# A linear-attention and routed-FFN kernel: one semaphore for each constant and load in the setup, and another order of its steps

## The reference

```python
q, k, v = split(x @ w_qkv)                      # to heads: 16 x 8
q_proj = elu1(einsum('bhnd,hdf->bhnf', q, proj))   # elu1(t) = t + 1 if t > 0 else exp(t)
k_proj = elu1(einsum('bhnd,hdf->bhnf', k, proj))
kv = einsum('bhnf,bhnd->bhfd', k_proj, v)
attn = einsum('bhnf,bhfd->bhnd', q_proj, kv) / (q_proj . sum_n(k_proj) + 1e-8)
x = layernorm(x + attn @ w_out + b_out)
expert = argmax(x @ wr + br)
x = layernorm(x + gelu(x @ w1[expert] + b1[expert]) @ w2[expert] + b2[expert])
```

## Time and profile before

| | us |
|---|---|
| runs | 243.63, 241.59, 245.2; median 243.63 |
| the profiled execution, its own time | 242.73 |
| its span in the trace | 241.0 |
| TensorE busy | 194.7 (81% of the span) |
| VectorE busy | 166.7 (69%) |
| ScalarE busy | 141.9 (59%) |
| GpSimd busy | 127.5 (53%) |

### The profile page before, as it was taken

One profiled execution on the slowest core, in us unless ns is written; L12 is line 12 of the kernel. 1 busy time (PEld: TensorE's weight loads), 2 busy tenths in 40 slices (PEclk: granted clock), 3 DMA queues, 4 the chain that ended last, 5 costly groups with the idle time before them and its releaser, 6 DMA issues.

```text
span 241.0 us, 5866 instructions
## 1 busy us (share of the span) xinstructions
PE 194.7 (81%) x1685; PEld 155.3 (64%) x1685; DVE 166.7 (69%) x539; ACT 141.9 (59%) x374; POOL 127.5 (53%) x161
## 2 busy tenths in 40 slices
PE   0778999999989889778874958899999899999100
PEld 0467887887854535444450447789999899999100
DVE  0247769686737789999998696767777757775600
ACT  2238888787846574675473356677766576676000
POOL 8203829273630012665585363644888756668860
PEclk9979999999999999999998579999999999999855
DMA  5999999998910000100110076861777887751100
GB/s 142 244 412 415 411 414 407 409 412 285 239 35 0 0 1 4 45 22 22 48 35 22 34 189 211 240 188 39 215 203 224 236 246 207 217 151 45 36 6 0
DMA packets 28416, 40.45 MB, mean 168 GB/s; under 512 B 3497, under 2 KB 18126, under 8 KB 28384
## 3 DMA queue, kind: packets, MB, share of 16 engines
q1 hardware_dynamic: 26112, 35.80, 45.4%
q0 software_dynamic: 2272, 4.27, 5.1%
HBM read 17.95 MB, written 22.56 MB: 168 GB/s over the span
## 4 chain that ended last, share of the span: by engine, by line
PE 47%; POOL 16%; issue 13%; DVE 11%; ACT 6%; DMA 2%; SPq 2%; DVEq 1%; ACTq 0%; POOLq 0%
PE pair L290 13%; PE pair L695 10%; PE pair L708 6%; POOL out_dram L493 5%; POOL sorted_rows L474 5%; PE bank L580 4%; PE bank L708 2%; PE pair L646 2%; DMA x_all<-sorted_rows 2%; POOL rstd L457 2%; PE pair L637 2%; PE bank L637 1%; PE pair L549 1%; DVE qexp L909 1%; POOL rstd L489 1%
## 5 line engine op out<-in xcount | busy, mean ns | idle before, releaser
L843 ACT ACTIVATE qfeat<-pair,w_sb 128x128 f32<-128x128 f32 x156 | 44.8, 369 | 26.1 <-PE pair L695 25.4
L695 PE MATMUL pair<-xsT,w_slot 128*128 128x128 f32 x312 | 42.6, 281 | 2.5 <-ACT xsT L833 1.6
L474 POOL DMA_INDIRECT sorted_rows<-x,dest x32 | 31.9, 997 | 17.7 <-issue 11.2
L695 PEld LDWEIGHTS pair<-xsT,w_slot 128*128 128x128 f32 x312 | 38.7, 195 | 3.7 <-issue 3.7
L290 PE MATMUL pair<-wkv_part,xT_all 128*128 128x256 f32 x192 | 34.6, 328 | 3.0 <-DVE xT_all L901 1.6
L290 PEld LDWEIGHTS pair<-wkv_part,xT_all 128*128 128x128 f32 x192 | 29.5, 195 | 6.4 <-issue 6.4
L502 POOL TENSOR_TENSOR ksum<-kfeat 128x512 f32<-128x512 f32 x12 | 16.3, 1355 | 31.8 <-DVE kfeat L918 31.8
L290 PE MATMUL pair<-xT_all,wq_part 128*128 128x512 f32 x96 | 31.8, 456 | 0.0
L708 PE MATMUL pair<-w_sb,qfeat 128*128 x232 | 30.8, 276 | 0.0
L797 ACT ACTIVATE qexp<-pair,minus_one 128x512 f32<-128x512 f32 x32 | 20.7, 680 | 15.5 <-PE pair L290 15.5
L493 POOL DMA_INDIRECT out_dram<-x_all x26 | 26.0, 1000 | 7.0 <-issue 5.8
(11 more groups left out here) (159 smaller groups left out, 362.3 us busy)
## 6 DMA issues: line engine op xcount, KB each, us to landing
sorted_rows<-pad_rows SPq DMA_DIRECT2D x11, 1584.0 KB, 23.0
w_slot<-in_L_ffn_w_dram SPq DMA_DIRECT2D x39, 256.0 KB
x_all<-in_L_attn_x_dram SPq DMA_DIRECT2D x8, 256.0 KB, 3.7
w_sb<-in_L_ffn_w_dram SPq DMA_DIRECT2D x4, 512.0 KB, 13.7
x_all<-sorted_rows SPq DMA_DIRECT2D x26, 66.0 KB, 2.6
xs<-sorted_rows SPq DMA_DIRECT2D x13, 66.0 KB, 2.7
w_sb<-in_L_ffn_b_dram SPq DMA_DIRECT2D x1, 512.0 KB, 6.8
sorted_rows<-x,dest POOLq DMA_INDIRECT x32, 2.4
```

What stands on the lines that cost most here:

```text
L474: g_.indirect_dma_start(out=sorted_rows, out_offset=bass.IndirectOffsetOnAxis(ap=dest[:, ring, i:i + 1], axis=0), in_=x1[:, ring, i, :], i ...
L695: last = mm(h_bank[t % 2][:, k * P:(k + 1) * P], w1_slot[:, t % WB, k * P:(k + 1) * P], xsT[:, t % 2, :], start=True, stop=True)
L843: a_.activation(hT[:, t % 2, k * P:(k + 1) * P], h_bank[t % 2][:, k * P:(k + 1) * P], ACT.Gelu, bias=w2_sb[:, bass.ds(w_at[t] + (FF + D + ...
```

## The change

GpSimd's constants get semaphores of their own (`ones_ready`, `ident_ready`, `mask_ready`, `pads_ready`), and so do the loads (`w_in`, `proj_in`, `wr_in`, `wout_in`). What makes the keys' weights goes first on every engine: the head mask's selects stand ahead of the other constants, and the fills of `pad_rows` and `x1` behind all. The query weights, the output weights and `b1` go behind the turning of x group 0, and the two score products (L553, L554 in the kernel before) between tiles 0 and 1. TensorE begins with four matmuls of ones into PSUM that nobody reads (`keep_awake`), and makes a fifth behind the first transposes. The core of the diff:

```diff
@@ sync @@
-            sp.dma_start(wqkv_sb[:, :], w_qkv).then_inc(const_in, 16)
-            sp.dma_start(proj_sb[:, :], proj.rearrange("h d f -> (h d) f")).then_inc(const_in, 16)
             def load_x(g):
                 sp.dma_start(x_all[:, g * GT:(g + 1) * GT, :], x_groups[g]).then_inc(x_loaded[g], 16)
+            sp.dma_start(wqkv_sb[:, :], w_qkv).then_inc(w_in, 16)
+            sp.dma_start(proj_sb[:, :], proj.rearrange("h d f -> (h d) f")).then_inc(proj_in, 16)
+            sp.dma_start(wr_sb[:, :], wr).then_inc(wr_in, 16)
             load_x(0)
+            sp.dma_start(wout_sb[:, 0:D], w_out).then_inc(wout_in, 16)
+            sp.dma_start(bout_col[:, :], b_out.rearrange("(d a) -> d a", a=1)).then_inc(wout_in, 16)
+            sp.dma_start(b1_rows[:, :], b1.rearrange("e (c p) -> (e c) p", p=P)).then_inc(b1_in, 16)
             load_x(1)
-            sp.dma_start(wout_sb[:, 0:D], w_out).then_inc(const_in, 16)
             sp.dma_start(bout_sb[:, :], b_out.rearrange("(a d) -> a d", a=1).to_broadcast([P, D])).then_inc(const_in, 16)
-            sp.dma_start(wr_sb[:, :], wr).then_inc(const_in, 16)
             sp.dma_start(br_sb[:, :], br.rearrange("(a d) -> a d", a=1).to_broadcast([P, E])).then_inc(const_in, 16)
-            sp.dma_start(bout_col[:, :], b_out.rearrange("(d a) -> d a", a=1)).then_inc(const_in, 16)
-            sp.dma_start(b1_rows[:, :], b1.rearrange("e (c p) -> (e c) p", p=P)).then_inc(b1_in, 16)
             for g in range(2, G):
...
-            sp.wait_ge(pool_consts, 1)
+            sp.wait_ge(pads_ready, 1)
@@ gpsimd @@
+            g_.memset(ones_bf[:, :], 1.0)
+            g_.memset(share[:, :], 1.0 / P).then_inc(ones_ready, 1)
             g_.memset(ident[:, :], 1.0).then_inc(zeroed, 1)
-            g_.memset(before[:, :], 1.0).then_inc(zeroed, 1)
             g_.memset(head_mask[:, :], 1.0).then_inc(zeroed, 1)
-            g_.memset(ones_bf[:, :], 1.0)
-            g_.memset(ones_kv[:, :], 1.0)
             g_.memset(mean_of[:, :], 1.0 / D)
-            g_.memset(den_eps[:, :], DEN_EPS)
             g_.memset(zero[:, :], 0.0)
             g_.memset(minus_one[:, :], -1.0)
-            g_.memset(share[:, :], 1.0 / P)
+            g_.memset(den_eps[:, :], DEN_EPS)
+            pool.wait_ge(zeroed, 2)
+            g_.affine_select(out=ident[:, :], in_=ident[:, :], compare_op=ALU.is_equal, fill=0.0, base=0,
+                             pattern=[[-1, P]], channel_multiplier=1).then_inc(ident_ready, 1)
+            g_.affine_select(out=head_mask[:, :], in_=head_mask[:, :], compare_op=ALU.is_ge, fill=0.0, base=0,
+                             pattern=[[-HD, H]], channel_multiplier=1).then_inc(zeroed, 1)
             g_.memset(block_mask[:, :], 1.0).then_inc(zeroed, 1)
+            g_.memset(before[:, :], 1.0).then_inc(zeroed, 1)
+            pool.wait_ge(zeroed, 3)
+            g_.affine_select(out=head_mask[:, :], in_=head_mask[:, :], compare_op=ALU.is_ge, fill=0.0, base=HD - 1,
+                             pattern=[[HD, H]], channel_multiplier=-1).then_inc(mask_ready, 1)
...
+            g_.iota(region_up[:, :], pattern=[[CAP, E]], base=1 - P, channel_multiplier=0,
+                    allow_small_or_imprecise_dtypes=True).then_inc(pool_consts, 1)
+            g_.memset(pad_rows[:, :, :], 0.0).then_inc(zeroed, 1)
+            pool.wait_ge(zeroed, 8)
+            g_.iota(pad_rows[:, :, D:D + 1].bitcast(I32), pattern=[[0, PR], [0, 1]], base=NO_TOKEN, channel_multiplier=0).then_inc(pads_ready, 1)
+            g_.memset(x1[:, :, :, :], 0.0).then_inc(zeroed, 1)
@@ tensor @@
-            pe.wait_ge(pool_consts, 1)
-            pe.wait_ge(const_in, 16 * 7)
+            def keep_awake(n):
+                for _ in range(n):
+                    mm(bank[5][:, :], ones_bf[:, :], share[:, :].to_broadcast([P, 512]), start=True, stop=True)
+            pe.wait_ge(ones_ready, 1)
+            keep_awake(4)
+            pe.wait_ge(ident_ready, 1)
+            pe.wait_ge(w_in, 16)
             for i in range(2):
                 nc.tensor.transpose(bank[0][:, i * P:(i + 1) * P], wqkv_sb[:, i * D:(i + 1) * D], ident[:, :]).then_inc(w_turned, 1)
-            mm(bank[3][:, 0:E], mean_of[:, :], wr_sb[:, :], start=True, stop=True).then_inc(wr_mean, 1)
-            nc.tensor.transpose(bank[4][:, 0:P], wout_sb[:, 0:D], ident[:, :]).then_inc(wout_turned, 1)
-            pe.wait_ge(b1_in, 16)
-            nc.tensor.transpose(bank[6][:, 0:E * FC], b1_rows[:, :], ident[0:E * FC, 0:E * FC]).then_inc(b1_turned, 1)
+            keep_awake(1)
             pe.wait_ge(w_turn_kept, 1)
             pe.wait_ge(proj_ready, 1)
-            for i in (1, 0):
-                mm(bank[1 + i][:, :], wT[:, i, :], proj_diag[:, :, :].rearrange("p h f -> p (h f)"),
-                   start=True, stop=True).then_inc(w_feat_pre, 1)
-            pe.wait_ge(woutT_ready, 1)
-            pe.wait_ge(wr_mid_ready, 1)
-            mm(bank[5][:, 0:E], woutT[:, :], wr_mid[:, :], start=True, stop=True)
-            mm(bank[5][:, E:2 * E], bout_col[:, :].to_broadcast([P, P]), wr_mid[:, :], start=True, stop=True).then_inc(wout_pre, 1)
+            def feature_weights(i, out):
+                mm(out, wT[:, i, :], proj_diag[:, :, :].rearrange("p h f -> p (h f)"), start=True, stop=True).then_inc(w_feat_pre, 1)
+            feature_weights(1, bank[2][:, :])
+            pe.wait_ge(wr_in, 16)
+            mm(bank[3][:, 0:E], mean_of[:, :], wr_sb[:, :], start=True, stop=True).then_inc(wr_mean, 1)
...
-                    pe.wait_ge(w_high, 3)
-                    pe.wait_ge(w_low, 3)
+                    pe.wait_ge(w_high, 2)
+                    pe.wait_ge(w_low, 2)
...
+            def other_weights():
+                feature_weights(0, bank[5][:, :])
+                pe.wait_ge(wout_in, 16 * 2)
+                nc.tensor.transpose(bank[4][:, 0:P], wout_sb[:, 0:D], ident[:, :]).then_inc(wout_turned, 1)
+                pe.wait_ge(b1_in, 16)
+                nc.tensor.transpose(bank[6][:, 0:E * FC], b1_rows[:, :], ident[0:E * FC, 0:E * FC]).then_inc(b1_turned, 1)
+            def score_weights():
+                pe.wait_ge(woutT_ready, 1)
+                pe.wait_ge(wr_mid_ready, 1)
+                mm(bank[4][:, P:P + E], woutT[:, :], wr_mid[:, :], start=True, stop=True)
+                mm(bank[4][:, P + E:P + 2 * E], bout_col[:, :].to_broadcast([P, P]), wr_mid[:, :], start=True, stop=True).then_inc(wout_pre, 1)
+            turn_group(0)
+            other_weights()
+            pe.wait_ge(pool_consts, 1)
+            for u in range(UT + 3):
                 if u > UB and u % UB == 2:
                     turn_kv(u // UB - 1)
                 if 0 <= u < UT:
                     keys_values(2 * u)
+                    if u == 0:
+                        score_weights()
                     keys_values(2 * u + 1)
                 if u % 2 == 0 and u // 2 + 1 < G:
                     turn_group(u // 2 + 1)
@@ scalar @@
             act.wait_ge(w_turned, 2)
             a_.copy(wT[:, :, :].rearrange("p a b -> p (a b)"), bank[0][:, 0:2 * P]).then_inc(w_turn_kept, 1)
-            act.wait_ge(wout_turned, 1)
-            a_.copy(woutT[:, :], bank[4][:, 0:P]).then_inc(woutT_ready, 1)
+            act.wait_ge(ident_ready, 1)
             a_.copy(wkv_part[:, 0, NF:NF + D], wqkv_sb[:, 2 * D:3 * D]).then_inc(w_high, 1)
-            for i in (1, 0):
-                act.wait_ge(w_feat_pre, 2 - i)
-                a_.copy((wq_part, wkv_part)[i][:, 0, 0:NF], bank[1 + i][:, :]).then_inc(w_high, 1)
-            act.wait_ge(pool_consts, 1)
+            def high_weights(part, of):
+                a_.copy(part[:, 0, 0:NF], of).then_inc(w_high, 1)
+            act.wait_ge(w_feat_pre, 1)
+            high_weights(wkv_part, bank[2][:, :])
...
-            for u in range(-2, UT + 2):
+            keep_xT(0)
+            act.wait_ge(w_feat_pre, 2)
+            high_weights(wq_part, bank[5][:, :])
+            act.wait_ge(wout_turned, 1)
+            a_.copy(woutT[:, :], bank[4][:, 0:P]).then_inc(woutT_ready, 1)
+            for u in range(UT + 2):
@@ vector @@
-            dve.wait_ge(pool_consts, 1)
-            dve.wait_ge(const_in, 16 * 7)
+            dve.wait_ge(mask_ready, 1)
+            dve.wait_ge(proj_in, 16)
             v.tensor_tensor(proj_diag[:, :, :], proj_sb[:, :].unsqueeze(1).to_broadcast([P, H, F]),
                             head_mask[:, :].unsqueeze(2).to_broadcast([P, H, F]), ALU.mult).then_inc(proj_ready, 1)
+            dve.wait_ge(w_high, 1)
+            v.tensor_tensor(wkv_part[:, 1, NF:NF + D], wqkv_sb[:, 2 * D:3 * D], wkv_part[:, 0, NF:NF + D].bitcast(F32),
+                            ALU.subtract).then_inc(w_low, 1)
+            def low_weights(part, of):
+                v.tensor_tensor(part[:, 1, 0:NF], of, part[:, 0, 0:NF].bitcast(F32), ALU.subtract).then_inc(w_low, 1)
+            dve.wait_ge(w_high, 2)
+            low_weights(wkv_part, bank[2][:, :])
...
-            for u in range(-2, UT):
+            low_part(0)
```

(40 more changed lines are left out.)

15 lines of the change are left out of this document (4 added, 11 removed).

## The result

| | before | after |
|---|---|---|
| runs, us | 243.63, 241.59, 245.2, 243.41 | 237.38, 235.65, 236.57, 235.08 |
| median, us | 243.52 | 236.11 |
| profiled execution, its own time | 242.73 | 237.38 |
| its span | 241.0 | 235.7 |

The ratio is 0.9728, 95% interval 0.9684 to 0.9772: the changed kernel is 2.7% faster. Its median of 236.11 lies 0.5 us from the forecast of 236.6.

What follows compares the result with a forecast made beforehand. The first 14.8 us are a serial setup chain behind one semaphore for all constants and one for all loads. Gain 6.5: 242.73 - 6.5 = 236.2, or 237.1 from the median; forecast 236.6 us, range 234.2 to 239.6.

Steps and rivals of the forecast that it cites:

- Start of the weights: Setup, TensorE's first weight transpose: waits for `w_qkv` alone, starts at 3.2 instead of 7.82 us, 4.6 us gained.
- Matmuls of ones at no cost: TensorE's start: four matmuls at 0.43 us each end at 2.9, before `w_qkv` lands; the fifth fits ScalarE's 0.4 us copy.
- My rise at 7.4: Setup: TensorE's clock rises at about 7.4 us, after 4.2 us of unbroken work from 3.2.
- `proj_diag` beside GpSimd, 0.4 us: VectorE in the setup: `proj_diag` beside GpSimd's selects pays between 0 and 0.7 us extra, taken as 0.4.
- The key product, 4.7 to 6.4: TensorE in the setup: the product for the key weights starts at 4.7 and ends at 6.4 us.
- Less the overlap: Key weights' product: two records at the low clock level, 2 x 0.91 us, shortened by their overlap.
- First product at 9.2: Start of the keys stage: the first product of keys starts at 9.2 instead of 14.79 us, 5.6 us gained.
- Tile 2 at 12.0: Keys stage: the product of tiles 2 and 3 starts at 12.0 instead of 18.56 us, 6.5 us gained in all.
- The rest: After tile 2: bulk fill still starts near 9.1 with 21 us left in hand; the whole gain reaches the end.
- The low clock: Rival: clock stays low through the first tiles, tile 2 at 14.9, gain 3.7, time 239.4 us; chance 0.13.
- The late input: Rival: x group 0 takes 1 us more or `proj_diag` the full 0.7; gain 5.2, time 237.9 us; chance 0.10.
- the whole gain reaches the end: From tile 2 on the engines' order is the same, so all 6.5 us hold to the last store.

Runs made afterwards that it cites:

- e3: Kernel before with only GpSimd's new order (masks first, large fills last); ratio 0.9997 (0.9937 to 1.0057).
- e7: Kernel before with only a semaphore for each load and each wait put where its data are used; ratio 0.9971 (0.9914 to 1.0028).
- e13: Kernel before with GpSimd's new order and all waits split, other engines' orders kept, no matmuls of ones; ratio 0.9978 (0.9945 to 1.001).
- e2: Changed kernel with the fills of x1 and pad_rows back ahead of GpSimd's first select; ratio 0.9809 (0.9713 to 0.9904).
- e1: Changed kernel without its five matmuls of ones; ratio 0.9713 (0.9603 to 0.9824), tile 2 at 12.96 us.
- e11: Second trace of e1, the changed kernel without matmuls of ones; one run, no ratio, tile 2 at 11.93 us.
- e5: Changed kernel with twelve instead of four matmuls of ones at the start; ratio 0.99 (0.9782 to 1.0018).
- e12: Second trace of e4, the changed kernel with query weights ahead of x; one run, no ratio, tile 2 at 13.10 us.
- e8: Changed kernel with VectorE's three router steps ahead of its low half of the key weights; ratio 0.982 (0.9701 to 0.9939).
- e9: Changed kernel once more, unaltered, on the chip of the experiments; ratio to the kernel before 0.9758 (0.9647 to 0.9868).
- e4: Changed kernel with query weights and transposes of w_out and b1 back ahead of turning x group 0; ratio 0.9887 (0.9767 to 1.0007).
- e10: Changed kernel with VectorE's router steps first, x1 fill held back, and matmuls of ones in three late TensorE pauses; ratio 0.9767 (0.9693 to 0.984).

## Why the prediction was right

**Start of the weights.** Gain 4.6 forecast, 4.38 measured (7.82 to 3.44); `w_qkv` was 2.5 us under way instead of 2.3. That it needs both waits split is shown by e3, e7 and e13. The price of the fills is shown by e2.

**Matmuls of ones at no cost.** Right: over at 2.98. Half of 0.91 is 0.46 and not the 0.43 that I took, though 0.43 is what the fifth one shows in the chain; and four more would by my own figures have put 1.4 us on the path, not 1.7. What I had not counted is that they bring the clock up sooner in most traces (e1, e11, e5). My rise at 7.4 had no term for them; in the changed kernel the record lengths turn near 7.

**`proj_diag` beside GpSimd, 0.4 us.** Mis-sized: it took 0.69 in the trace of the changed kernel, as alone. The larger price fell on GpSimd, whose select L438 took 0.94. With VectorE idle beside it the same select took 0.64 (e3; L431 in the kernel before). Nobody waits for that select. The other traces show that `proj_diag` was not free of GpSimd either. It meets the select before, recorded from 3.11 to 3.76; in e13 it started sooner and took longer. From the timelines of e13 and e3:

```profile
3.44 0.78 DVE L885 TENSOR_TENSOR proj_diag<-proj_sb,head_mask 128x512 f32<-128x512 f32 x1 [3.44 <-DMA proj_sb<-_L_attn_proj_matrix_dram]
3.83 0.64 POOL L432 TENSOR_SCALAR_AFFINE_SELECT block_mask<-block_mask 128x256 f32<-128x256 f32 x1
```

Started at 3.44, 3.45, 3.49 and 3.51 (e13, e12, e8, e9), `proj_diag` took 0.78, 0.76, 0.72 and 0.72 and was over at 4.21 to 4.23 each time; from 3.54 on it took 0.69. So when it started sooner, it seems to have been held until about 3.53, which is 0.2 us ahead of the recorded end of the select. The select behind it ended 0.50 or 0.51 us after `proj_diag` in each of these traces and in that of the changed kernel.
By the Trainium skill ("SBUF — State Buffer", Who interferes with whom) the later of two such instructions waits for the earlier. Both ends agree with it. By this reading `proj_diag` paid nothing in the changed kernel because `proj` landed just as the select let go. The same section says that a cast can run in a mode in which it contends with GpSimd, and e8 agrees with that: 1.09 us against 0.17.

**The key product, 4.7 to 6.4.** It ran from 4.56 to 6.65. "Less the overlap" was mis-sized: two records at the low level took 2.09, so 0.91 for each was short and there is no overlap worth a term.

**First product at 9.2.** Measured 9.21, but by another path. I let it end with x (TensorE, ScalarE, VectorE) and found 9.1, and put TensorE's queue at 9.0. ScalarE had x's half ready at 8.16; VectorE was still at the key weights and the three router steps and started x's low half at 8.38. My sum had no wait for VectorE's own row. TensorE's queue was through at 8.7, not 9.0. Errors of 0.2 to 0.4 us in the single terms cancelled, so that the start was met to 0.01 us is luck; the serial chain it stands on is not. e4 and e12 price the order of the query weights: 1.3 us.

**Tile 2 at 12.0.** Measured 11.86 and 11.79; both tiles and the turn ran at the high level, the 0.34 us of the score products stood as read. The turn took 0.35 from its start to tile 2 (11.51 to 11.86), not 0.5.

**The rest.** The gain at the first scatter was 6.4 of 6.5. The bulk fill did not start near 9.1 but at 10.60, since six issues of x took 4.9 us and not 3.4; its end moved from under 68 to just over it, still over 20 us ahead of the first scatter, so nothing followed. A near miss that I had not named: the load of `br`, moved behind x group 1, was 4.6 us under way and landed at 9.8, and VectorE needs it at 11.1.

**Rivals.** The low clock was seen once (e4), in another order. The late input did not come, and of the gain 1.2 us, not all, were lost behind the first up-product, against my step that the whole gain reaches the end. My sum for the profiled execution was 236.2, and it took 237.38; the median of the four came to 236.11. The median gained 7.4 us where the traces gained 5.3: the profiled execution of the changed kernel was the slowest of its four, and before's was below its median. So the nearness of 236.1 to 236.6 is in part the luck of the executions. The lower end of my range, 234.2, does not follow from the lower of the two baselines (242.73 - 7.4 = 235.3) but from the fastest run, 241.59. The longer low stretch between 133 and 144 is a candidate for the difference between 6.5 at the first up-product and 5.3 at the end. That it is the cause was not shown: e10's shorter stretch brought nothing at the end, on a chip with another expert stage.
